# VectorE's order in the third step of an attention block: two row-weight remainders and a value remainder moved behind maxima and low halves

## The reference, cut to what matters

```python
x = x + layernorm(attn(layernorm(x)))      # x: 2 batches x 512 tokens x 512
x = x + layernorm(ffn(layernorm(x)))       # gated mixture beside a base product

# attn, 32 heads of 128, INNER = 4096
q = rms_norm(h @ Wq + bq, gq); k = rms_norm(h @ Wk + bk, gk); v = h @ Wv + bv
attn = softmax(einsum('bhqd,bhkd->bhqk', q, k) / sqrt(128))
out = einsum('bhqk,bhkd->bhqd', attn, v) ; return out @ Wo + bo
```

## Time and profile before

| | us |
|---|---|
| median of 3 timed runs | 1068.48 (1067.88 to 1068.65) |
| the profiled execution's own time | 1073.24 |
| its span | 1071.4 |
| TensorE busy | 1044.0 (97%) |
| VectorE busy | 821.3 (77%) |
| ScalarE busy | 762.6 (71%) |
| GpSimd busy | 761.5 (71%) |

### The profile page before, as it was taken

One profiled execution on the slowest core, in us unless ns is written; L12 is line 12 of the kernel. 1 busy time (PEld: TensorE's weight loads), 2 busy tenths in 40 slices (PEclk: granted clock), 3 DMA queues, 4 the chain that ended last, 5 costly groups with the idle time before them and its releaser, 6 DMA issues.

```text
span 1071.4 us, 19670 instructions
## 1 busy us (share of the span) xinstructions
PE 1044.0 (97%) x5649; PEld 551.4 (51%) x5649; DVE 821.3 (77%) x1824; ACT 762.6 (71%) x1582; POOL 761.5 (71%) x717
## 2 busy tenths in 40 slices
PE   8999999999999989999999999999999999999897
PEld 5444444444445645556555555555555555544454
DVE  7888766667746778766787887787887887888887
ACT  3676666666657776776787788687787788677756
POOL 2688978788868466775777877877778778645513
PEclk8999999999999999999999999999999999999999
DMA  6679765656664679866577887867878878776702
GB/s 239 172 238 273 258 221 197 230 206 228 205 137 139 199 177 241 236 157 177 138 163 206 183 163 199 165 177 187 194 167 186 197 185 173 210 164 148 186 22 80
DMA packets 312409, 198.86 MB, mean 186 GB/s; under 512 B 275456, under 2 KB 279424, under 8 KB 312320
## 3 DMA queue, kind: packets, MB, share of 16 engines
q1 hardware_dynamic: 304688, 194.24, 68.0%
q10 hardware_dynamic: 7632, 3.57, 1.3%
HBM read 94.98 MB, written 35.68 MB: 122 GB/s over the span
## 4 chain that ended last, share of the span: by engine, by line
PE 80%; DVE 8%; ACT 5%; issue 3%; DMA 2%; POOL 1%; SPq 0%; ACTq 0%; POOLq 0%; DVEq 0%
PE ps L1594 24%; PE ps L1595 23%; PE ps L1596 23%; PE ps L1786 3%; PE ps L1788 3%; PE ps L1787 3%; DVE pair_q L2515 3%; ACT ps L1288 2%; ACT pair_q L1297 1%; DMA pair_k<-pair_q 1%; DVE ps L2501 1%; ACT k_hi L1245 1%; DVE stats L2090 1%; DMA y<-x 0%; DVE ffn_top L2619 0%
## 5 line engine op out<-in xcount | busy, mean ns | idle before, releaser
L2515 DVE SCALAR_TENSOR_TENSOR pair_q<-ps,row_inv,pair_q 128x512 f16<-128x512 f32 x256 | 174.5, 745 | 68.6 <-ACT pair_q L1297 65.0
L1288 ACT ACTIVATE ps<-ps,neg_max 128x512 f32<-128x512 f32 x256 | 168.2, 657 | 76.1 <-DVE ps L2501 76.0
L1594 PE MATMUL ps<-xh,wa_hi 128*128 128x512 f16 x512 | 194.2, 379 | 0.0
L1596 PE MATMUL ps<-xh,wa_lo 128*128 128x512 f16 x512 | 194.2, 379 | 0.0
L1595 PE MATMUL ps<-xl,wa_hi 128*128 128x512 f16 x512 | 194.2, 379 | 0.0
L2501 DVE TENSOR_SCALAR_CACHE_REDUCE ps<-ps,score_down 128x512 f32<-128x512 f32 x256 | 177.0, 753 | 12.2 <-PE ps L1596 11.9
L1297 ACT ACTIVATE pair_q<-ps,row_inv 128x512 f16<-128x512 f32 x256 | 154.5, 688 | 7.8 <-DVE row_inv L2508 7.5
L742 POOL TENSOR_TENSOR acc<-acc,squares 128x512 f32<-128x512 f32 x120 | 151.5, 1284 | 1.6 <-ACT squares L1139 1.6
L1139 ACT ACTIVATE squares<-ps,q_k_bias,qk_down 128x512 f32<-128x512 f32 x128 | 99.3, 784 | 45.9 <-PE ps L1596 31.6
L733 POOL TENSOR_TENSOR qk_out<-q_s,qk_out 128x512 f16<-128x512 f32 x64 | 76.0, 1188 | 53.3 <-ACT qk_out L1148 53.3
L2300 DVE TENSOR_SCALAR qk_out<-ps,k_b,k_g 128x512 f32<-128x512 f32 x64 | 51.8, 809 | 77.1 <-ACT squares L1139 77.1
(11 more groups left out here) (310 smaller groups left out, 2578.3 us busy)
## 6 DMA issues: line engine op xcount, KB each, us to landing
q_k_scratch<-qk_out SPq DMA_DIRECT2D x64, 512.0 KB, 3.6
qk_in<-q_k_scratch SPq DMA_DIRECT2D x64, 512.0 KB, 3.7
wa_stage<-w_qk SPq DMA_DIRECT2D x32, 512.0 KB, 4.3
u_stage<-w_vo SPq DMA_DIRECT2D x32, 512.0 KB, 5.3
wo_stage<-w_vo SPq DMA_DIRECT2D x16, 512.0 KB, 5.2
x_first<-w_vo SPq DMA_DIRECT2D x12, 512.0 KB, 4.5
qk_tops<-qk_top_scratch ACTq DMA_DIRECT2D x27, 128.0 KB, 3.7
y<-x SPq DMA_DIRECT2D x8, 256.0 KB, 6.0
```

The source lines that it names most:

```text
L1288: act.activation(ps[:, SCORE + i, :], ps[:, SCORE + i, :], ACT.Exp, bias=neg_max[:, sl, i:i + 1], scale=-1.0, accum_out=row_sum[:, sl, i:i ...
L1594: pe.matmul(outp, lhs[0], rhs[0], start=first, stop=False)
L1596: return pe.matmul(outp, lhs[1], rhs[0], start=False, stop=last)
L2515: dve.scalar_tensor_tensor(out=pair_q[:, 1, i, :], in0=ps[:, SCORE + i, :], scalar=row_inv[:, sl, i:i + 1], in1=pair_q[:, 0, i, :], op0=AL ...
```

## The change

The diff writes VectorE's calls of the third step in another order. Nothing is added or removed, no operand changes, and the programs of the other engines and queues are the same in both kernels.

```diff
             scores_down(2, 0, 0, 1)
             first_low_k(1)
+            maxima(2, 0)
             low_wo(0)
-            maxima(2, 0)
-            low_wo(1)
             inverses(2, 0)
-            split_v(4, 6, YB)
             for i in range(TB):
                 low_halves(2, 0, i)
+            split_v(4, 6, YB)
+            low_wo(1)
             scores_down(3, 1, 1, 1)
             step(0, 3, 0, plain, rows=False)
```

## The result

The changed kernel takes 1075.52 us (median of 6, 1074.17 to 1076.39), the kernel before 1068.57 us (median of 6, 1067.88 to 1070.60). The ratio is 1.006, 95% interval 1.0051 to 1.007, so it is slower by 6.4 us (5.4 to 7.5). The forecast was slower, by 3.3 us.

The account below looks back on a forecast made before the run. TensorE was taken as the bound, its stop and slow clock at `attend(2)` worth 3.95 us. Later transposes (2.9) plus clock (0.4) gave +3.3 us on 1068.48, so 1071.8 us, range 1069.8 to 1075.0.

Parts of the forecast that it names:

- The early maxima and the first `low_wo`: VectorE, step 2: maxima start 0.69 us earlier, at 375.55; `low_wo(0)` behind them is hidden before the reciprocal.
- The values' remainder: VectorE's `split_v` behind the low halves: gains nothing, and its reader, the row products, starts no earlier for other reasons.
- The end T of the second `low_wo`: VectorE, step's end: T between 384.5 and 385.5, taken as 385.0, against 379.66 before; later bound if GpSimd contends.
- The hold of the SP queue and the megabyte ahead: SP queue held until T, then 1 MB ahead of transposes: second lands at T + 8.5, TensorE starts 2.9 us later.
- Rival B: Queue held, but transposes not queued behind the loads: landing at T + 7.16, +1.05 to +2.1 us; chance 0.13.
- A stop of this kind should be the same in both: Profiled and timed runs, 4.8 us apart, have the same TensorE stop, so +3.3 us is added to 1068.48.
- the fall of the clock: TensorE in `attend(2)`: clock already falls before the change, so the extra is 0.4 us, at most 1.04.
- rival C: Transfer pause: recurring, near +5.4 us; second half, absent from timed runs before, up to 6.3 us, 1074.8; chance 0.19.
- Side chains: ScalarE's rounding waits for the late load, cover about 5 us, priced at nothing; row products' delay up to 0.5 hidden.
- Rival D: Faster: earlier maxima reach the transposes if T is at or before 381.2; up to 3.7 us gained; chance 0.06.

Follow-up runs that it names:

- e1: Kernel before with only the second `low_wo` moved to the end of the step, behind the low halves; ratio 1.0077, +8.2 us.
- e9: Kernel before with the first `low_wo` moved up ahead of the first keys of batch 1; ratio 0.9993 (0.9985 to 1.0002).
- e2: Changed kernel with the second `low_wo` put right behind the inverses, ahead of the low halves; ratio 1.0002.
- e6: Changed kernel, ScalarE's rounding behind step 3's value copy; SP queue still waits for both `low_wo` but loads row weights behind step 2's transposes; ratio 1.0036.
- e7: Kernel before, ScalarE's rounding behind step 3's value copy; SP queue issues both loads only once step 2's high halves are ready; ratio 1.0057.
- e0: Kernel before, unchanged, run again for a second profile; 1068.64 us, ratio 1.0001.
- e5: Changed kernel with only ScalarE's rounding of the new row weights moved behind step 3's value copy; ratio 1.0059.
- e3: Changed kernel with the SP queue's load of row weights issued behind the two transposes of step 2; ratio 1.0063.
- e11: The kernel of e9 measured again; ratio 0.9993 (0.9982 to 1.0004).
- e10: Changed kernel with 44 idle-time matmuls of constants added on TensorE between the row products and `attend(2)`; ratio 1.0096, +10.3 us.

## Why the prediction was right in direction and too small

*The early maxima and the first `low_wo`*: right, maxima at the scores' pace, `low_wo(0)` at 0.75 us and hidden. What that is worth in time no pair of runs shows clearly (e1, e9).

*The values' remainder*: right, costs nothing (e2).

*The end T of the second `low_wo`*: forecast 14.4 us behind the last transpose of step 1 (385.0, with that transpose at 370.64), with 13.9 as the early bound; measured 383.50 - 369.77 = 13.73, just ahead of the early bound. VectorE's instruction kept its 0.74 us, and the meeting with GpSimd, for which the later bound was there, was paid on the other side, by its cast, which took 1.19 us instead of 0.61:

```profile
382.78 1.19 POOL L919 CAST oth<-o_t 128x512 f16<-128x512 f32 x1 [1.46 <-ACT o_t L1262]
```

*The hold of the SP queue and the megabyte ahead*: right, and shown by e1, e6 and e7. Forecast: first transpose issued at T + 1.38, measured 1.39; it lands 2.1 us behind the key load, measured 2.1; second lands at T + 8.5, measured 392.99 - 383.50 = 9.5, since the key load took 5.1 us and not 4.2. That and the earlier T nearly cancel, by luck: the landing was forecast 22.9 us behind the mark, measured 23.2. What I had not seen is where the wait is served: not in the transfer but in the issue, 4.09 us of the queue, so that the second transpose goes out at T + 5.6 instead of T + 3.16. The sign was in the earlier trace rows: that issue took 2.62 us and ended at 590.74, with the load's landing at 590.8, but I read the landings only. Rival B, in which transposes pass the loads, fell.

*"A stop of this kind should be the same in both"*: this is the step that failed. The profiled execution of before had a pause in its second transpose that e0's profile does not have, and the timed runs are too short to have it as a rule. From e0 the landing is at 385.38 + 4.1 = 389.5, 18.6 behind its mark, not 20.0. So the delay of `attend(2)` is 4.64 us and not 2.9, and the fall of the clock, which I counted as already paid, is new: 2.19 us and not 0.4. (Even against the first profile it was 4.77 - 4.13 = 0.64; four of the twelve matmuls were fast there, not three, and one in the changed kernel.) The sum with these two is 6.83, and the timed loss 6.4. The second half of rival C said just this, at 6.3 us and 1074.8; I had given it too little, with a profiled execution 4.8 us above the median as the sign, and the range ended at 1075.0, 0.5 us below the measured median. On the base that the forecast used, the ratio gives 1068.48 x 1.006 = 1074.9; that the range reached so far is luck, since its sum was half of what the change costs.

*Side chains*: the row products started 0.6 us later than before (at +15.53 instead of +14.95), which the idleness behind them hid, as forecast. ScalarE's chain was priced at nothing with 5 us of cover for `attend(3)`. Cutting it gives nothing back that e5 could show (1.0059 against 1.006), but I had named the wrong reader. The first to want step 3 is the scores of step 4, by the low halves, with 2.1 us of cover and not 5, and e3 shows this chain to be worth the full loss as soon as the transposes are not late. The two chains run side by side and are nearly as long, which is why curing either alone gives nothing back.

*Rival D*: excluded; T was far too late. In e9 its 0.7 us do reach the transposes.

## What to carry to other kernels

Before moving an instruction back, find every queue that waits for its semaphore, a DMA queue above all, and list what that queue issues next: here a remainder of weights, wanted by TensorE only for products with idle time behind them, held a queue with urgent transposes in it. A bulk load that is issued right ahead of a short urgent transfer is paid for even where nothing holds the queue: in e7 two loads of 512 KB sent the second transpose out 2.8 us late. And when the profiled execution is further from the median than the runs are from each other, take a second profile of the same kernel before forecasting from its waits.

## What the runs showed of the hardware

Issuing the first transposing transfer of step 2 took the SP queue 1.7 us with the last load issued 3.2 us ahead (before, e0; 1.91 in e11), 2.3 us with it 1.9 us ahead (e2), 2.70 us right behind 512 KB (e6), and 3.64 to 4.95 us right behind 1 MB (the changed kernel, e1, e5, e7, e10). Where a load was less than 3 us ahead, these issues have their end in common, 0.1 to 0.4 us ahead of the landing of the key load: at 388.98 and 389.0 in the changed kernel, 390.45 and 390.8 in e1, 383.83 and 384.2 in e2, 388.90 and 389.1 in e6, 387.75 and 388.1 in e7. So it looks as if the issue waits for the load ahead to be nearly through; no run was made to try just that.

Where VectorE's `low_wo(1)` and GpSimd's cast of 128 x 512 met at the end of the step, the one that started second took longer. In the changed kernel VectorE was first by 0.02 us, with 0.74 us against 1.19 for the cast; in e1 GpSimd was first by 0.04 us, with 0.61 for the cast and 1.11 for VectorE.

The pause in the first profile has a companion. The transfers of the core in that stretch, GB/s in 40 slices, and the one instruction-fetch packet in it:

```profile
GB/s 236 264 295 528 268 268 272 272 252 260 232 87 24 0 0 0 0 0 0 0 0 0 0 0 8 8 8 8 12 8 12 8 12 8 12 8 8 91 280 288
q8 instruction: 1, 0.02, 3.2%
```

The same stretch in e0, where no such packet falls:

```profile
GB/s 240 284 295 268 295 288 288 295 280 299 288 280 291 288 288 288 264 288 272 276 252 398 284 56 106 457 146 142 378 126 63 315 189 315 378 252 252 378 126 378
```

In the first, the rate falls to nearly nothing for some 1.5 us in the middle of the transpose, with the fetch of 16 KB of instructions in the same stretch; in e0 the transpose runs through. In e10 one such packet again falls into the transposes of step 2 and the second lands 5.2 us after issue, and in e1 one falls into the first transpose's issue of 4.95 us. In step 3 the first transpose's issue took 2.28 us in the changed kernel, 3.38 in e5, 3.15 in e6 and 2.98 in e7, with the last load 2.1 to 3.0 us ahead and one such packet in each; in e0, where the packet falls just ahead of that transpose's issue, it took 1.89. That a fetch which meets a transpose pauses it is only argued from these; no run tried it.
